# Placing the shift rows of the softmax: from SyncE's queue to ScalarE's, with two transfers of four rows for each group of heads

## The chip, the cores and the metric

The kernel runs on one core of one Trainium2 chip. The metric is the device time of one execution in microseconds (us). A core has five engines, each with its own instruction stream: TensorE (matrix products), VectorE, ScalarE, GpSimd and SyncE (here it only issues DMAs). They wait for each other by semaphores. A DMA is issued by an instruction in the stream of some engine: if an earlier instruction of that stream waits, the issue waits too.

## The reference

One transformer block on 16 sequences of 512 tokens by 512 channels, in float32:

```python
x = x + layernorm(attention(layernorm(x)))     # 32 heads of 16, causal, rotary, biases on q, k, v, o
x = x + layernorm(ffn(layernorm(x)))           # 512 -> 1408 -> 512, silu(gate) * up, ternary weights with scales
```

Inside the attention the weights are softmax(q k^T / 4) over the keys up to the query's position.

## The kernel before

There are two phases, one after the other. The attention (`attention_phase`) goes over the 16 sequences and writes its result to DRAM; the feed-forward part then reads it. The change is in the attention alone.

**Steps.** A sequence has NS = 40 steps: NG = 8 groups g of four heads, each with NU = 5 units u, so step s = 5 g + u. Each engine has a `body(i)` that lists its work for the 40 steps in a fixed order, written out by hand. In it lie, interleaved, work of three sequences: projections of the next sequence, the attention of this one, the output of the one before. Sequences 1 to 13 are passes of a hardware loop; the first and the last ones are written out.

**Heads in slots.** Each head of q and k is held as 64 rows (a slot, SLOT = 64): 48 rows are the 16 dimensions three times over, as high and low float16 halves, and 16 (DH) are constant rows. Two heads (j = 0, 1) stand one above the other in the 128 partitions of `qT` and `kT`; the first index behind the partition is the channel tile ct = g // 2, the second the pair of heads. The halves come from VectorE and are sent to a DRAM buffer `slots` (`send_slots`, four DMAs), then read back in the new order (`fetch_slots`, two DMAs of 256 KB), since rows have to change partitions. Both stand in SyncE's queue. A fetch waits until its sends have landed. The constant rows of k hold 32768 (SHIFT_UNIT), those of q hold 0. They are written to DRAM once, in the set-up.

**Maxima and shift.** Ten steps ahead (AHEAD) of its use, TensorE computes the scores with queries in the partitions (`maxima`, line 799), and VectorE masks them and takes their row maxima (line 674). After the five units of a group, VectorE makes two float16 numbers of each maximum, divided by -32768 (`shift_of_maxima`). At u = 1 of the group before, TensorE turns them into rows (`turn_shift`, line 837), eight rows of 512: four heads, a high and a low one each. ScalarE copies them from PSUM to the tile `shift_rows` (`read_shift`, line 532). Then they are put in two of the constant rows of each head's slot in `qT`, over zeros: `place_shift`, lines 362 to 371, four DMAs of 2 KB at u = 2 in SyncE's queue. The second product, with keys in the partitions (`transposed_scores`, line 813), so has the shift in it, and ScalarE can exponentiate at once (`exponential`, line 526). At u = 0 of a group the second product waits for the shift rows:

```python
                if u == 0:
                    pe.wait_ge(shift_in, 64 * (NG * i + g + 1))
                wait_if_any(pe, ts_read, NS * i + n)
```

The second product has one buffer, `ts`: the next unit's can't start before ScalarE has read it (`ts_read`). The first product has two, `mx`.

**Order on SyncE.** In each step: the placement (u = 2), then a fetch, then a send, then now and then a load or a store of a whole sequence (1 MB). Fetches stand in steps 0, 1, 6, 10, 25, 26, 31 and 35, sends in steps 0, 5, 9, 24, 25, 30, 34 and 39. The key slots of the first channel tile are fetched in step 26 and wanted in step 30.

**Order on ScalarE.** In each step the exponential; a bias (`add_bias`, line 513); a high half (`high_of_roped`, line 520); at u = 1 `read_shift`; at u = 2 the copy of the weighed values (`read_weighed`, line 536), for which TensorE's `turn_weighed` waits; then copies of transposed tiles.

Of the kernel before, what the change touches and what calls it, by code (L numbers as in the profile page):

```python
# [45 lines left out]
def held(engine, value):  # L46

    return value if isinstance(value, int) else engine.to_reg(value)


def wait_if_any(engine, semaphore, value):

    if not isinstance(value, int) or value > 0:
        engine.wait_ge(semaphore, value)
# [16 lines left out]
def attention_phase(nc, x, wT, bias_rows, bias_columns, rope_cos, rope_sin, slots, x1):  # L71

    ctx = ExitStack()
    with ctx:
# [124 lines left out]
        SCALES_AT = 2 + SCALE_STEPS  # L199


        NS = NG * NU
        AHEAD = 2 * NU

# [96 lines left out]
        def exists(i):  # L301

            return not isinstance(i, int) or 0 <= i < NB
# [17 lines left out]
        @block.sync  # L321
        def _(sp):
            sp.dma_start(xn[:, :, :], x[0, :, :, :]).then_inc(x_in, 16)
            for n in range(4):
                sp.dma_start(staged[:, n, :, :], wT[n]).then_inc(weights_in[n], 16)
            for n in range(2):
                sp.dma_start(bias_sb[:, n, :], bias_rows[n]).then_inc(tables_in, 16)
            sp.dma_start(bias_columns_sb[:, :, :], bias_columns).then_inc(tables_in, 16)
            sp.dma_start(cos_sb[:, :], rope_cos).then_inc(tables_in, 16)
            sp.dma_start(sin_sb[:, :], rope_sin).then_inc(tables_in, 16)  # L330
            sp.dma_start(xr[:, :, :], x[0, :, :, :]).then_inc(xr_in, 16)
            sp.wait_ge(padding, 4)
            for n in range(2):
                sp.dma_start(slots[n, :, 3 * DH:SLOT, :].rearrange("jp r t -> r jp t"),
                             half[0:SLOT - 3 * DH, n, 0:1, :].broadcast_to([SLOT - 3 * DH, 8, T])).then_inc(pads_out, 16)

            def send_slots(i, n):

                ct, which = divmod(n, 2)
                b = n % 2  # L340
                halved, fetched = held(sp, 8 * i + n + 1), held(sp, 32 * (NC * i + ct))
                sp.wait_ge(qk_lo, halved)
                wait_if_any(sp, k_in if which else q_in, fetched)
                rows = slots[which, :, 0:3 * DH, :].rearrange("jp (e d s) t -> e jp d (s t)", e=2, s=3)
                both_at, high_at = ((slice(0, 2 * T), slice(2 * T, 3 * T)), (slice(T, 3 * T), slice(0, T)))[which]
                for e in range(2):
                    part = slice(64 * e, 64 * e + 64)
                    sp.dma_start(rows[e][:, :, both_at], half[part, b, :, :]).then_inc(slots_out, 16)
                    sp.dma_start(rows[e][:, :, high_at], half[part, b, 0, :]).then_inc(slots_out, 16)

            def fetch_slots(i, n):

                ct, which = divmod(n, 2)
                dst, arrived = ((qT, q_in), (kT, k_in))[which]
                sp.wait_ge(slots_out, 64 * (8 * i + n + 1))
                if isinstance(i, int) and i == 0 and n < 2:
                    sp.wait_ge(pads_out, 32)
                for j in range(2):
                    sp.dma_start(dst[SLOT * j:SLOT * (j + 1), ct, :, :],
                                 slots[which, 4 * j:4 * j + 4, :, :].rearrange("p r t -> r p t")).then_inc(arrived, 16)  # L360

            def place_shift(i, g):

                turned_rows, placed = held(sp, NG * i + g + 1), held(sp, 64 * (NG * i + g))
                sp.wait_ge(shift_read, turned_rows)
                wait_if_any(sp, shift_in, placed)
                for j in range(2):
                    for pair in range(2):
                        at = 4 * j + 2 * pair
                        sp.dma_start(qT[SLOT * j + 3 * DH:SLOT * j + 3 * DH + 2, g // 2, 2 * (g % 2) + pair, :],  # L370
                                     shift_rows[at:at + 2, g % 2, :]).then_inc(shift_in, 16)

            def body(i):
                for s in range(NS):
                    g, u = divmod(s, NU)
                    if u == 2 and exists(i + (g + 1) // NG):
                        place_shift(i + (g + 1) // NG, (g + 1) % NG)
                    if s in FETCHED_AT and exists(i + FETCHED_AT[s][1]):
                        fetch_slots(i + FETCHED_AT[s][1], FETCHED_AT[s][0])
                    if s in SENT_AT and exists(i + SENT_AT[s][1]):  # L380
                        send_slots(i + SENT_AT[s][1], SENT_AT[s][0])
                    if s == 16 and exists(i + 1) and (not isinstance(i, int) or i + 2 < NB):
                        sp.wait_ge(xT_full, NC * (i + 2))
                        sp.dma_start(xn[:, :, :], x[i + 2, :, :, :]).then_inc(x_in, 16)
                    if s == 26 and exists(i - 1):
                        sp.wait_ge(x1_ready, NT * i)
                        sp.dma_start(x1[i - 1, :, :, :], xr[:, :, :]).then_inc(x1_out, 16)
                    if s == 28 and exists(i - 1) and exists(i):
                        sp.wait_ge(x1_out, 16 * i)
                        sp.dma_start(xr[:, :, :], x[i, :, :, :]).then_inc(xr_in, 16)  # L390

            body(-1)
            body(0)
            with sp.Fori(1, NB - 2) as i:
                body(i)
            body(NB - 2)
            body(NB - 1)
            body(NB)
            sp.wait_ge(x1_out, 16 * NB)
# [100 lines left out]
        def _(act):  # L500
# [26 lines left out]
                                     scale=exp_scale[:, 0:1]).then_inc(ts_read, 1)  # L527

            def read_shift(i, g):
                wait_if_any(act, shift_in, 64 * (NG * i + g - 1))  # L530
                act.wait_ge(shift_full, NG * i + g + 1)
                nc.scalar.activation(shift_rows[0:8, g % 2, :], xb16[0:8, bank_of("s", g), 0:T], ACT.Copy).then_inc(shift_read, 1)

            def read_weighed(i, g):
                act.wait_ge(av_full, NG * i + g + 1)
# [2 lines left out]
            def body(i):  # L538
                for s in range(NS):
                    g, u = divmod(s, NU)  # L540
                    if u == 0 and s in BIASED_AT and exists(i + BIASED_AT[s][1]):
                        add_bias(i + BIASED_AT[s][1], BIASED_AT[s][0])
                    if exists(i):
                        exponential(i, g, u)
                    if u != 0 and s in BIASED_AT and exists(i + BIASED_AT[s][1]):
                        add_bias(i + BIASED_AT[s][1], BIASED_AT[s][0])
                    if s in HIGH_AT and exists(i + HIGH_AT[s][1]):
                        high_of_roped(i + HIGH_AT[s][1], HIGH_AT[s][0])
                    if u == 1 and exists(i + (g + 1) // NG):
                        read_shift(i + (g + 1) // NG, (g + 1) % NG)  # L550
                    if u == 2 and exists(i + (g - 1) // NG):
                        read_weighed(i + (g - 1) // NG, (g - 1) % NG)
                    if s in TRANSPOSED_AT and exists(i + TRANSPOSED_AT[s][2]):
                        kind, c, owner = TRANSPOSED_AT[s]
                        (high_of_x if kind == "x" else high_of_attention)(i + owner, c)

            act.wait_ge(setup_step, SCALES_AT)
            for n in range(4):
                nc.scalar.activation(w_hi[:, n, :, :], staged[:, n, :, :], ACT.Copy,
                                     scale=scale[:, n:n + 1]).then_inc(weights_hi, 1)  # L560
            act.wait_ge(pads_out, 32)
            act.wait_ge(setup_done, 4)
            body(-1)
            body(0)
# [7 lines left out]
        def _(dve):  # L572
# [93 lines left out]
            def maxima(i, n):  # L666
                g, u = divmod(n, NU)
                filled = held(dve, NS * i + n + 1)
                dve.wait_ge(consts, 7)
                dve.wait_ge(mx_full, filled)  # L670
                for pair, qt, at in QUERIES_OF_UNIT[u]:
                    for j in range(2):
                        scores = mx[:, 2 * (n % 2) + j, at:at + P * (qt + 1)]
                        last = nc.vector.tensor_tensor_reduce(  # L674
                            out=scores, in0=scores, in1=causal[:, T - P * (qt + 1):T], scale=1.0, scalar=-3e38,
                            op0=ALU.add, op1=ALU.max, accum_out=row_max[:, g % 2, qt, j, pair:pair + 1])
                last.then_inc(mx_read, 1)

            def shift_of_maxima(i, g):
# [103 lines left out]
        def _(pe):  # L783
# [20 lines left out]
            def transposed_scores(i, n):  # L804
                g, u = divmod(n, NU)
                ct = g // 2
                if u == 0:
                    pe.wait_ge(shift_in, 64 * (NG * i + g + 1))
                wait_if_any(pe, ts_read, NS * i + n)
                for pair, kt, at in KEYS_OF_UNIT[u]:  # L810
                    for j in range(2):
# [567 lines left out]
```

## Time and profile before

| | |
|---|---|
| median of 3 runs | 3089.23 us |
| the three runs | 3087.83, 3089.23, 3095.59 us |
| the profiled execution: its time | 3092.81 us |
| its span, first to last instruction | 3091.1 us |
| mean granted clock of TensorE | 0.938 |
| attention phase, shift placements | first 90.9 us, last 2017.3 us |
| shift placements | 512 DMAs of 2.0 KB |

The profile is of one execution. Its page gives the busy time of each engine; other views give what an engine waited for, the instructions in order of time with the idle time before each and what ended it, and busy time by stretch. PE is TensorE's matrix products, DVE is VectorE, ACT ScalarE, POOL GpSimd, SPq SyncE's queue. Line numbers are those of the kernel before. The granted clock is 1.00 at 2.4 GHz and 0.50 at 1.2 GHz.

### The profile page before, as it was taken

To read this page: it belongs to the slowest core of one execution; us is meant where nothing else is said; L and a number is where in the kernel's file an instruction comes from. 1 tells how busy PE (TensorE), PEld (TensorE's weight loads), DVE (VectorE), ACT (ScalarE), POOL (GpSimd) and SP (SyncE) were. 2 spreads that over 40 slices of the span, in tenths; PEclk is the share of its full clock that TensorE was granted. 3 is DMA by queue.
4 is the path that set the end of the run, shared out by engine and by line. 5 is a ranking of instruction groups with operands and counts; after the bars stand their busy time and mean duration, and the time that the engine had idled before them with its cause. 6 is when DMAs were issued, how large, how long until landed. Compare 5 with 4: busy or idle time off the path is not lost. (4 is left out here: it accounts for less than half of the span.)

```text
span 3091.1 us, 58855 instructions
## 1 busy us (share of the span) xinstructions
PE 2605.4 (84%) x19584; PEld 1263.9 (41%) x19584; DVE 2202.2 (71%) x6495; ACT 1330.2 (43%) x1710; POOL 1020.9 (33%) x1051
## 2 busy tenths in 40 slices
PE   3788888888888888888888888843999999999997
PEld 2343434444434444444444444311444444444443
DVE  4888878788788887887888888836555555545544
ACT  2455555555545555555555555524222222222222
POOL 3454455454544644545446545310000000000000
PEclk9899999999899998998999999876999999999999
DMA  3222232322332323223223232221111111111111
GB/s 140 83 78 90 83 94 63 108 90 64 109 92 77 98 63 104 90 63 111 91 75 97 71 96 77 75 116 56 42 54 41 68 53 42 68 41 54 68 41 41
DMA packets 125076, 237.06 MB, mean 77 GB/s; under 512 B 11408, under 2 KB 94608, under 8 KB 111632
## 3 DMA queue, kind: packets, MB, share of 16 engines
q1 hardware_dynamic: 124816, 233.63, 23.8%
q8 instruction: 158, 2.59, 0.4%
q14 instruction: 102, 0.84, 0.1%
HBM read 148.39 MB, written 84.15 MB: 75 GB/s over the span
## 5 line engine op out<-in xcount | busy, mean ns | idle before, releaser
L674 DVE CUSTOM_DVE_ANT_0 mx<-mx,causal 128x512 f32<-128x512 f32 (+3 forms) x2048 | 944.3, 517 | 245.8 <-PE mx L799 243.5
L526 ACT ACTIVATE probs<-ts,exp_scale 128x1024 f32<-128x1024 f32 x640 | 712.5, 1113 | 714.3 <-PE ts L813 713.9
L452 POOL TENSOR_SCALAR_AFFINE_SELECT probs<-probs 128x512 f32<-128x512 f32 x512 | 320.7, 644 | 782.1 <-ACT probs L526 782.1
L1219 DVE SCALAR_TENSOR_TENSOR hidden<-gu,up_scale,silu 128x512 f32<-128x512 f32 x176 | 131.9, 749 | 418.4 <-PE gu L1269 418.4
L1078 ACT ACTIVATE silu<-gu,gate_scale 128x512 f32<-128x512 f32 x176 | 120.9, 687 | 631.7 <-PE gu L1269 631.7
L799 PE MATMUL mx<-kT,qT 64*128 64x512 f16 (+3 forms) x2048 | 262.6, 315 | 153.5 <-DMA kT<-slots 70.0
L1053 POOL TENSOR_TENSOR f_rstd<-f_var,f_neg_half 128x4 f32<-128x4 f32 x32 | 32.3, 1009 | 929.6 <-DVE f_var L1196 647.5
L813 PE MATMUL ts<-qT,kT 64*128 64x512 f16 (+3 forms) x2048 | 257.5, 310 | 74.2 <-DMA qT<-shift_rows 61.8
L1267 PE MATMUL gu<-f_xT_hi,gate_hi 128*128 128x512 f16 x704 | 267.9, 381 | 52.2 <-issue 52.2
L827 PE MATMUL xb<-probs,vs 128*32 128x512 f32 (+3 forms) x4096 | 309.7, 444 | 1.4 <-POOL probs L452 1.1
L674 DVE DVE_READ_ACCUMULATOR2_ANT row_max<- 128x1 f32 x2048 | 283.3, 138 | 0.0
L1269 PE MATMUL gu<-f_xT_lo,gate_hi 128*128 128x512 f16 x704 | 267.8, 380 | 0.0
L1267 PE MATMUL gu<-f_xT_hi,up_hi 128*128 128x512 f16 x704 | 267.3, 380 | 0.0
L1269 PE MATMUL gu<-f_xT_lo,up_hi 128*128 128x512 f16 x704 | 267.1, 379 | 0.0
L1281 PE MATMUL down<-down_hi,hid_hi 128*128 128x512 f16 x704 | 266.8, 379 | 0.0
L1285 PE MATMUL down<-down_hi,hid_lo 128*128 128x512 f16 x704 | 266.8, 379 | 0.0
L431 POOL TENSOR_TENSOR turned<-biased,sin_sb 64x512 f32<-64x512 f32 x128 | 193.2, 1509 | 161.8 <-ACT biased L513 159.4
L785 PE MATMUL xb<-xT_hi,w_hi 128*128 128x512 f16 x512 | 205.4, 401 | 14.6 <-DVE aT_lo L645 10.3
L799 PEld LDWEIGHTS mx<-kT,qT 64*128 64x128 f16 x2048 | 69.3, 94 | 356.5 <-issue 242.9
L785 PE MATMUL xb<-w_hi,xT_hi 128*128 128x128 f16 x1024 | 207.1, 238 | 5.3 <-DVE aT_lo L645 4.5
L786 PE MATMUL xb<-w_lo,xT_hi 128*128 128x128 f16 x1024 | 206.8, 238 | 0.0
L787 PE MATMUL xb<-w_hi,xT_lo 128*128 128x128 f16 x1024 | 206.1, 238 | 0.0
(145 smaller groups left out, 4607.4 us busy)
## 6 DMA issues: line engine op xcount, KB each, us to landing
slots<-half SPq DMA_DIRECT2D x258, 128.0 KB, 13.7
qT<-slots SPq DMA_DIRECT2D x128, 256.0 KB, 3.8
kT<-slots SPq DMA_DIRECT2D x128, 256.0 KB, 3.8
xn<-x SPq DMA_DIRECT2D x16, 1024.0 KB, 4.9
xr<-x SPq DMA_DIRECT2D x16, 1024.0 KB, 5.8
slots<-half SPq DMA_DIRECT2D x256, 64.0 KB
x<-xr SPq DMA_DIRECT2D x16, 1024.0 KB, 5.6
f_xn<-x SPq DMA_DIRECT2D x16, 1024.0 KB, 4.8
```

What stands on the lines that cost most here:

```text
L452: nc.gpsimd.affine_select(out=d, in_=d, compare_op=ALU.is_ge, fill=0.0, base=0, pattern=[[0, HG], [1, P]], channel_multiplier=-1).then_inc ...
L526: nc.scalar.activation(probs[:, g % 2, u, :, :], ts[:, :, :], ACT.Exp, scale=exp_scale[:, 0:1]).then_inc(ts_read, 1)
L674: last = nc.vector.tensor_tensor_reduce(out=scores, in0=scores, in1=causal[:, T - P * (qt + 1):T], scale=1.0, scalar=-3e38, op0=ALU.add, o ...
L785: nc.tensor.matmul(out, a_hi, b_hi, start=first, stop=False)
L786: nc.tensor.matmul(out, a_hi, b_lo, start=False, stop=False)
L799: last = nc.tensor.matmul(mx[:, 2 * (n % 2) + j, at:at + P * (qt + 1)], qT[rows, ct, p, P * qt:P * (qt + 1)], kT[rows, ct, p, 0:P * (qt + ...
L813: last = nc.tensor.matmul(ts[:, j, at:at + T - P * kt], kT[rows, ct, p, P * kt:P * (kt + 1)], qT[rows, ct, p, P * kt:T], start=True, stop= ...
L827: last = nc.tensor.matmul(bank[32 * h:32 * h + 32, P * kt:T], vs[:, g // 2, kt, HG * (g % 2) + h, :], probs[:, g % 2, u, j, at:at + T - P ...
L1267: nc.tensor.matmul(gu[:, bank, :], hi[:, c, cols], xT_hi[:, c, :], start=c == 0, stop=False)
L1269: last = nc.tensor.matmul(gu[:, bank, :], hi[:, c, cols], xT_lo[:, c, :], start=False, stop=end and not with_rest)
L1281: nc.tensor.matmul(down[:, t, :], hid_hi[:, b % 3, rows], down_hi[:, b, :], start=b == 0, stop=False)
L1285: last = nc.tensor.matmul(down[:, t, :], hid_lo[:, b % 3, rows], down_hi[:, b, :], start=False, stop=b == NI - 1)
```

## The change

The shift rows are issued by ScalarE, at u = 1, directly behind its copy of them, after a wait for that copy. For this the rows of a pair of heads, even and odd, have to be four adjacent partitions of `qT`: the even head's slot gets its constant rows at its end (partitions 48 to 63), the odd head's at its beginning (64 to 79), so that partitions 62 to 65 (`SHIFT_ROWS`) take them. In DRAM a slot has 80 rows, constants on both sides of the data, and a fetch takes rows 16 to 79 or 0 to 63 (`ROWS_OF`). The maxima are stored with the pair ahead of j, so that the eight rows come in this order. The constant rows are sent by four DMAs of 16 rows in place of two.

```diff
+        ROWS_OF = (slice(DH, DH + SLOT), slice(0, SLOT))
+        SHIFT_ROWS = slice(SLOT - 2, SLOT + 2)
...
             for n in range(2):
-                sp.dma_start(slots[n, :, 3 * DH:SLOT, :].rearrange("jp r t -> r jp t"),
-                             half[0:SLOT - 3 * DH, n, 0:1, :].broadcast_to([SLOT - 3 * DH, 8, T])).then_inc(pads_out, 16)
+                for first in (0, SLOT):
+                    sp.dma_start(slots[n, :, first:first + DH, :].rearrange("jp r t -> r jp t"),
+                                 half[0:DH, n, 0:1, :].broadcast_to([DH, 8, T])).then_inc(pads_out, 16)
...
-                rows = slots[which, :, 0:3 * DH, :].rearrange("jp (e d s) t -> e jp d (s t)", e=2, s=3)
+                rows = slots[which, :, DH:SLOT, :].rearrange("jp (e d s) t -> e jp d (s t)", e=2, s=3)
...
-                                 slots[which, 4 * j:4 * j + 4, :, :].rearrange("p r t -> r p t")).then_inc(arrived, 16)
-
-            def place_shift(i, g):
-
-                turned_rows, placed = held(sp, NG * i + g + 1), held(sp, 64 * (NG * i + g))
-                sp.wait_ge(shift_read, turned_rows)
-                wait_if_any(sp, shift_in, placed)
-                for j in range(2):
-                    for pair in range(2):
-                        at = 4 * j + 2 * pair
-                        sp.dma_start(qT[SLOT * j + 3 * DH:SLOT * j + 3 * DH + 2, g // 2, 2 * (g % 2) + pair, :],
-                                     shift_rows[at:at + 2, g % 2, :]).then_inc(shift_in, 16)
+                                 slots[which, 4 * j:4 * j + 4, ROWS_OF[j], :].rearrange("p r t -> r p t")).then_inc(arrived, 16)
...
-                    if u == 2 and exists(i + (g + 1) // NG):
-                        place_shift(i + (g + 1) // NG, (g + 1) % NG)
...
+            def place_shift(i, g):
+                act.wait_ge(shift_read, NG * i + g + 1)
+                wait_if_any(act, shift_in, 32 * (NG * i + g))
+                for pair in range(2):
+                    act.dma_start(qT[SHIFT_ROWS, g // 2, 2 * (g % 2) + pair, :],
+                                  shift_rows[4 * pair:4 * pair + 4, g % 2, :]).then_inc(shift_in, 16)
...
                         read_shift(i + (g + 1) // NG, (g + 1) % NG)
+                        place_shift(i + (g + 1) // NG, (g + 1) % NG)
...
-                            op0=ALU.add, op1=ALU.max, accum_out=row_max[:, g % 2, qt, j, pair:pair + 1])
+                            op0=ALU.add, op1=ALU.max, accum_out=row_max[:, g % 2, qt, pair, j:j + 1])
...
-                    pe.wait_ge(shift_in, 64 * (NG * i + g + 1))
+                    pe.wait_ge(shift_in, 32 * (NG * i + g + 1))
...
-    slots = nc.dram_tensor("slots", (2, 8, SLOT, T), F16, kind="Internal").ap()
+    slots = nc.dram_tensor("slots", (2, 8, SLOT + DH, T), F16, kind="Internal").ap()
```

The waits for `shift_in` and `pads_out` elsewhere have their counts changed to match.

## Rows read from the trace of the kernel before

**Rows 1.** The page: busy us (share of the span) and instructions by engine.
```profile
PE 2605.4 (84%) x19584; PEld 1263.9 (41%) x19584; DVE 2202.2 (71%) x6495; ACT 1330.2 (43%) x1710; POOL 1020.9 (33%) x1051
```

**Rows 2.** What TensorE waited for: us in total, times, longest us.
```profile
PE mx L799 <- DMA kT<-slots: 70.0, 15, 9.7
PE ts L813 <- DMA qT<-shift_rows: 61.8, 30, 5.7
PE mx L799 <- issue: 54.3, 14, 6.2
...
PE ts L813 <- ACT probs L526: 11.7, 15, 1.3
```

**Rows 3.** TensorE in order of time: start us, us, instruction, [idle before <-releaser].
```profile
110.83 0.61 PE L813 MATMUL ts<-qT,kT 64*128 64x512 f16 x2 [5.67 <-DMA qT<-shift_rows]
...
302.43 0.61 PE L813 MATMUL ts<-qT,kT 64*128 64x512 f16 x2 [2.25 <-DMA qT<-shift_rows]
...
1036.98 0.61 PE L799 MATMUL mx<-kT,qT 64*128 64x512 f16 x2 [3.87 <-DMA kT<-slots]
...
1039.56 0.61 PE L813 MATMUL ts<-qT,kT 64*128 64x512 f16 x2 [1.97 <-DMA qT<-shift_rows]
...
1085.00 0.61 PE L813 MATMUL ts<-qT,kT 64*128 64x512 f16 x2 [4.25 <-DMA qT<-shift_rows]
...
1457.20 0.39 PE L813 MATMUL ts<-qT,kT 64*128 64x512 f16 x2 [1.10 <-DMA qT<-shift_rows]
...
1904.35 0.61 PE L813 MATMUL ts<-qT,kT 64*128 64x512 f16 x2 [2.07 <-DMA qT<-shift_rows]
...
1948.70 0.61 PE L813 MATMUL ts<-qT,kT 64*128 64x512 f16 x2 [4.34 <-DMA qT<-shift_rows]
```

**Rows 4.** SyncE's queue in order of time, steps 26, 27 and 40 to 42.
```profile
1032.04 1.28 SPq L359 DMA_DIRECT2D kT<-slots  x2
...
1034.07 3.75 SPq L370 DMA_DIRECT2D qT<-shift_rows  x4
...
1072.07 1.30 SPq L359 DMA_DIRECT2D qT<-slots  x2
1073.59 0.62 SPq L348 DMA_DIRECT2D slots<-half  x1
...
1079.20 1.86 SPq L359 DMA_DIRECT2D kT<-slots  x2
1081.25 2.58 SPq L370 DMA_DIRECT2D qT<-shift_rows  x4
```

**Rows 5.** ScalarE in order of time: step 27, then steps 41 and 42.
```profile
1025.77 1.11 ACT L526 ACTIVATE probs<-ts,exp_scale 128x1024 f32<-128x1024 f32 x1 [2.90 <-PE ts L813]
...
1071.83 0.57 ACT L532 ACTIVATE shift_rows<-xb 8x512 f16<-8x512 f16 x1
1073.08 1.11 ACT L526 ACTIVATE probs<-ts,exp_scale 128x1024 f32<-128x1024 f32 x1 [0.68 <-PE ts L813]
1074.10 0.68 ACT L513 ACTIVATE biased<-xb,bias_qk 128x512 f32<-128x512 f32 x1
1075.40 0.60 ACT L536 ACTIVATE oT<-xb 128x512 f32<-128x512 f32 x1 [0.62 <-PE xb L827]
```

**Rows 6.** Line 370, the placement: duration ns minimum/median/maximum, first and last start us.
```profile
L370 SPq DMA_DIRECT2D qT<-shift_rows x512: 562/563/1568, 90.9 to 2017.3; - x171
```

**Rows 7.** VectorE in order of time, behind the waits of 1039.56 and 1085.00 us.
```profile
1043.25 0.70 DVE L674 CUSTOM_DVE_ANT_0 mx<-mx,causal 128x512 f32<-128x512 f32 x1 [2.95 <-PE mx L799]
...
1088.98 0.70 DVE L674 CUSTOM_DVE_ANT_0 mx<-mx,causal 128x512 f32<-128x512 f32 x1 [3.87 <-PE mx L799]
```

**Rows 8.** Stretches, step 5 to 10: us; PE, PEld, DVE, ACT, POOL busy; clock; DMA.
```profile
1080.40:1099.70 19.30, 14.70 (x139) 8.52 (x140) 14.49 (x52) 8.44 (x11) 8.22 (x10) 0.82 0.29 76
1455.70:1470.20 14.50, 12.33 (x139) 6.97 (x138) 14.15 (x52) 8.60 (x11) 8.30 (x10) 1.00 0.25 66
```

**Rows 9.** A stretch around step 30: us; TensorE busy; granted clock; DMA share, GB/s.
```profile
1035.80:1042.60 6.80, 3.65 (x28) 0.50 0.67 241
```

**Rows 10.** TensorE's second product of step 43 (u = 3).
```profile
1075.49 0.38 PE L813 MATMUL ts<-qT,kT 64*128 64x384 f16 x4
```

More of the change, by code:

```diff
@@ L356, in fetch_slots @@
                 if isinstance(i, int) and i == 0 and n < 2:
-                    sp.wait_ge(pads_out, 32)
+                    sp.wait_ge(pads_out, 64)
                 for j in range(2):
                     sp.dma_start(dst[SLOT * j:SLOT * (j + 1), ct, :, :],
-                                 slots[which, 4 * j:4 * j + 4, :, :].rearrange("p r t -> r p t")).then_inc(arrived, 16)
-            def place_shift(i, g):
-                turned_rows, placed = held(sp, NG * i + g + 1), held(sp, 64 * (NG * i + g))
-                sp.wait_ge(shift_read, turned_rows)
-                wait_if_any(sp, shift_in, placed)
-                for j in range(2):
-                    for pair in range(2):
-                        at = 4 * j + 2 * pair
-                        sp.dma_start(qT[SLOT * j + 3 * DH:SLOT * j + 3 * DH + 2, g // 2, 2 * (g % 2) + pair, :],
-                                     shift_rows[at:at + 2, g % 2, :]).then_inc(shift_in, 16)
+                                 slots[which, 4 * j:4 * j + 4, ROWS_OF[j], :].rearrange("p r t -> r p t")).then_inc(arrived, 16)
             def body(i):
@@ L529, in read_shift @@
             def read_shift(i, g):
-                wait_if_any(act, shift_in, 64 * (NG * i + g - 1))
+                wait_if_any(act, shift_in, 32 * (NG * i + g - 1))
                 act.wait_ge(shift_full, NG * i + g + 1)
                 nc.scalar.activation(shift_rows[0:8, g % 2, :], xb16[0:8, bank_of("s", g), 0:T], ACT.Copy).then_inc(shift_read, 1)
+            def place_shift(i, g):
[4 more added lines that the diff above has]
+                                  shift_rows[4 * pair:4 * pair + 4, g % 2, :]).then_inc(shift_in, 16)
             def read_weighed(i, g):
@@ L560, in _ @@
                                      scale=scale[:, n:n + 1]).then_inc(weights_hi, 1)
-            act.wait_ge(pads_out, 32)
+            act.wait_ge(pads_out, 64)
             act.wait_ge(setup_done, 4)
```

## The prediction
> **What bounds the kernel now.** I read the shares of the page first. TensorE is busy 84% of the span, VectorE 71%, ScalarE 43% [rows 1]. No engine is full, so the time is made of work plus waits on TensorE and VectorE, which run nearly level; ScalarE has room. The second view is what TensorE waited for [rows 2]. Three entries stand out: 70.0 us for the key slots (15 times), 61.8 us for the shift rows (30 times) and 54.3 us with no releaser (14 times, at the return to the loop's head). Only the second is touched by this change.
>
> The third view is where the 30 waits lie [rows 3]. One in each sequence comes at step 30, just after the wait for the key slots: 2.25 us in the first row of this kind, 1.97 at 1039.56 us, 2.07 in the last, so 15 of about 2.0 make some 30 us. The other 32 us lie in the other 15 waits, nearly all at step 5 (a new group of heads, g = 1), and they are uneven: 1.10 us at 1457.20, 4.25 at 1085.00, 5.67 and 4.34 in the first and last large ones. Seven are above 2 us, about 27 us together.
>
> The fourth view is SyncE's queue around such a wait [rows 4]. The shift rows were ready early: ScalarE began the copy at 1071.83 and it took 0.57 us, so 1072.40 [rows 5]. But SyncE issued them only at 1081.25: ahead in its order stood a fetch of query slots (1072.07), four sends (from 1073.59), and a fetch of key slots, which could not go before its sends had landed (1079.20). The four transfers took 2.58 us to issue, and TensorE started at 1085.00, 1.17 us after the last. At step 30 it is the same: the placement stands behind a fetch of key slots and a store, from 1034.07, and took 3.75 us. So the shift rows are late because they queue on SyncE, not because they are slow.
>
> **The change, part by part.**
>
> Taken from SyncE: 4 issues for each of 128 groups, 512 x 563 ns = 288 us [rows 6], and its wait for the copy. SyncE's other work is bound by halves coming from VectorE and by landings. The fetch that makes the 70.0 us wait (step 26) has no placement between itself and its two sends, so I give the 288 us no value. The bounds are 0 and, if the fetch moved up by one placement, 2.58 us x 15 = 39 us gained [rows 2, 4]; I take 0.
>
> The wait that goes: with the placement on ScalarE directly behind the copy, the rows are issued from 1072.40. Two issues and the 1.17 us landing put them in qT at about 1074.7, where TensorE wants them at 1080.75 (1085.00 less 4.25). That is 6 us to spare. All 30 waits go. What they were worth is not the same at both places:
> - Step 30: behind the wait VectorE was idle as well, 2.95 us before its next block of maxima at 1043.25 [rows 7]. So TensorE's 1.97 us moves VectorE forward too. 15 x 2.0 = 30 us. If VectorE took it back, as at the next place, 0 to 10 would be left.
> - Step 5: VectorE is behind TensorE there. The stretch from the maxima of step 5 to those of step 10 takes 14.5 us where the stall was 1.10 us, with VectorE busy 14.15 of it, and 19.3 us where it was 4.25, with VectorE busy 14.49 [rows 8]. So 14.5 us is the floor, set by VectorE; the small stalls cost nothing, and a large one gives back somewhat more than itself (19.3 - 14.5 = 4.8), since the clock was at its lower level after it (0.82 against 1.00 in these two rows). For the seven large ones, 27 us of wait, I take 24 us, as some of it is below the floor. The small ones: 0.
>
> The clock: around step 30 there is a stretch of 6.8 us at 0.50, the 1.2 GHz level, with TensorE busy 3.65 us in it [rows 9]. It begins in the wait for the key slots, which stays, but the wait that goes lies in its middle. If the clock is back up for all that work, 3.65 / 2 = 1.8 us is saved, in 15 sequences 27 us; if it is not, 0. Nearest to a sequence like that is the same one with its key wait of 3.87 us still there, so I take the low end, 0.5 us each, 8 us.
>
> What of the late 4.25 us is issue time? SyncE's four issues took 2.58 us, from 1081.25, and stood 8.85 us behind the copy's end [rows 4, 5]; two issues on ScalarE take 1.13. The Trainium skill speaks against the change here: "DMA: Bandwidth & Descriptors", in "Rules for kernel authors", says that spreading DMAs over the issuing engines does not help bandwidth, as all run on the same 16 DMA engines, and saves issue time only. By that rule alone the sum would hold nothing but the issue time (rival C); by the rows the larger part is what stands ahead in SyncE's order, a fetch that waits for its sends.
>
> Added to ScalarE: a wait for its own copy and two issues, at each of 128 groups, in front of the exponential of step u = 2. No ScalarE issue stands in this trace. The lower bound is 0 (where the engine would have been idle anyhow); the nearest row is SyncE's issue of the same kind, 563 ns, and the far end is its longest, 1568 ns [rows 6]. I take 563 ns and 0.1 us for the wait for the copy: 1.23 us. In a tight group ScalarE stands idle 0.68 us between the copy and that exponential, which comes 0.55 us late. Behind it are queued a bias (0.68 us) and the copy of the weighed values, which now waits 0.62 us for TensorE [rows 5]: the 0.55 is just swallowed. On TensorE's side, the scores of step u = 3 start at 1075.49 [rows 10], and this exponential ends at 1074.19: 1.30 us of room against 0.55. In other groups the exponential waits longer for TensorE anyhow, 2.90 us in one [rows 5]; I count five of eight as tight. For trifles above the cover I put 0.3 us per sequence, 5 us. With 1568 ns issues it is 3.24 us, the exponential 2.56 late, and TensorE 1.3 to 1.9 us late in some five of eight groups: 1.6 x 5 x 16 = 128 us lost. That is the upper bound of the cost.
>
> The other edits: the fetched block has the same 64 rows of 1 KB, now from a stride of 80 rows; the maxima are written at other addresses of the same small tile; the constant rows are sent by four transfers in place of two, during the set-up, while ScalarE is busy with the weights. 0; the set-up could lose a microsecond.
>
> Sum: 30 + 24 + 8 - 5 = 57 us of the profiled execution's 3092.81 us (span 3091.1): 3036. The median of before is 3089.23, 3.6 us lower, and the profiled execution lies inside the three runs (3087.83 to 3095.59). I forecast 3036 us.
>
> **The rivals.**
>
> A. VectorE takes the gain back at step 30 as it does at step 5. For it: it was busy 71% over the whole and has 14.15 of 14.5 in the stretch shown. Against: its 2.95 us idle right behind the wait. It would leave 24 + a third of 30, less 5: 29 us, so 3063.
>
> B. The other side: ScalarE's issues are slow. The place is the exponential of u = 2, on the single score buffer that TensorE refills. The price is 128 us less the 62 gained: 3158 us at the far end. It decides where 62 us are lost in 80 tight groups, 0.78 us each: a stay of 0.68 + 0.62 + 0.78 = 2.08 us for wait and issues, 1.0 us an issue. Against it: median and minimum of 512 issues are 563 and 562 ns.
>
> C. The shift rows still come late, since they share the DMA engines with the slot traffic, and only issue time is saved: 2.58 - 1.13 = 1.45 us [rows 4, 6] at each of 22 large waits (15 + 7), 32 us, less 5: 3066. For it: one placement took 3.75 us at 1034.07, behind other traffic [rows 4]. Against: the 6 us to spare. The skill's rule above would have it so.
>
> D. The clock gives more: stretches at the low level disappear at step 30 too, and the key slots' wait is shorter with SyncE free. 57 + 20 to 30: 3010.
>
> **How the numbers follow.** The forecast 0.55, its own range 3025 to 3048. A 0.13, B 0.07, C 0.10, D 0.15. The range 3008 to 3072 holds the forecast, D, A and most of C. What a measurement can tell from no change is 0.3%, 9 us. Slower than 3098: nearly all of B, 0.07. Within 9 us: the edges of B and C, 0.05. Faster: 0.88.
>
> **What would show it.** TensorE's wait for shift rows falls from 61.8 us to under 5, its wait for key slots stays near 70, and the one at the loop's head near 54. The stretch from step 5 to step 10 is 14.5 us in each sequence. SyncE issues no shift rows; ScalarE has 256 issues of about 0.56 us. TensorE's waits for the exponentials, now 11.7 us [rows 2], stay under 20. I am wrong if the issues on ScalarE last over 1 us, if the key-slot wait grows by what the shift wait loses, or if VectorE's share of a sequence is at its limit.

## The result, and the profile after

The changed kernel takes 3050.51 us, the median of 4 runs (3043.4 to 3056.82), against 3088.9 us before on the same occasion. The ratio is 0.9871 (95% interval 0.984 to 0.9901): 1.3% faster, about 40 us, 31 to 49 by the interval. Forecast were 3036 us and a range of 3008 to 3072. The median lies in that range, 2.5 us above the narrower one that the prediction gave the forecast itself (3025 to 3048). The profiled execution took 3045.72 us, 47.1 us under the one before, and 4.8 us under the median of its kernel; what the profile shows has to be read with that in mind.

The page after, where [rows 1] stands before:

```profile
PE 2582.9 (85%) x19584; PEld 1250.2 (41%) x19584; DVE 2205.0 (72%) x6495; ACT 1328.8 (44%) x1710; POOL 1023.4 (34%) x1051
```

What TensorE waited for (us in total, times, longest us), to be held against [rows 2]:

```profile
PE mx L799 <- DMA kT<-slots: 74.6, 14, 9.3
PE mx L799 <- issue: 57.2, 15, 6.5
...
PE xb L785 <- DVE aT_lo L645: 30.5, 34, 2.0
...
PE xb L860 <- DVE attn L699: 12.7, 26, 1.0
PE ts L813 <- ACT probs L518: 11.5, 13, 1.3
```

What matters is what isn't there: no row for the shift rows, 61.8 us before. The waits for the key slots and at the loop's head are where they were. Waits for small results of VectorE took some of the room (`aT_lo` was 16.3 us).

What VectorE waited for, of the two kernels; first before, then after:

```profile
DVE mx L674 <- PE mx L799: 243.5, 200, 12.5
...
DVE roped L651 <- ACT biased L513: 15.8, 41, 5.4
```

```profile
DVE mx L674 <- PE mx L799: 180.1, 136, 12.1
...
DVE roped L651 <- ACT biased L505: 33.4, 38, 5.3
```

VectorE starves less behind TensorE, by 63 us, and waits 17.6 us longer for ScalarE's bias, a row that the prediction had not looked at.

The placement on ScalarE (line 530): duration ns minimum/median/maximum. Then ScalarE in order of time in steps 41 and 42, to be held against [rows 5]:

```profile
L530 ACTq DMA_DIRECT2D qT<-shift_rows x256: 584/595/1182, 83.1 to 1965.9; - x128
```

```profile
1046.61 0.57 ACT L524 ACTIVATE shift_rows<-xb 8x512 f16<-8x512 f16 x1
1047.29 1.29 ACTq L530 DMA_DIRECT2D qT<-shift_rows  x2
1048.69 1.11 ACT L518 ACTIVATE probs<-ts,exp_scale 128x1024 f32<-128x1024 f32 x1 [1.51 <-DMA qT<-shift_rows]
1049.71 0.68 ACT L505 ACTIVATE biased<-xb,bias_qk 128x512 f32<-128x512 f32 x1
1050.32 0.60 ACT L535 ACTIVATE oT<-xb 128x512 f32<-128x512 f32 x1
```

The issues last 595 ns, the stay between copy and exponential is 1.51 us, and the copy of the weighed values no longer waits for TensorE: the 0.62 us of cover before it is used up.

Where the time went, by sequence. The table is worked out from the starts of line 799's products at the steps named, as means over the 12 sequences from the third on, 299.6 to 1777.8 us before and 291.7 to 1741.1 us after:

| us | step 30 to 31 | 31 to 40, loop's head | 0 to 5 | 5 to 10 | 10 to 20 | 20 to 30 | sum | of it at the low clock |
|---|---|---|---|---|---|---|---|---|
| before | 5.73 | 26.26 | 13.52 | 15.40 | 29.02 | 33.25 | 123.18 | 16.5 |
| after | 3.54 | 26.24 | 14.29 | 14.53 | 28.72 | 33.45 | 120.78 | 11.6 |

Step 30 gave back 2.19 us and steps 5 to 10 0.87, but steps 0 to 5 took 0.77 us of it. Those 12 sequences hold 28.8 us of the 47.1; the rest lies in the first and last ones, which had large stalls too. Over all sequences, worked out in the same way, step 30 gave 31.1 us and steps 5 to 10 gave 25.2, steps 0 to 5 took 12.4, and everything else together gave 3.2.

### The profile page after: what moved, and what is told of

It is laid out like the page before. It is cut to its first block and busy times, and to the rows that moved or that the text cites. A ratio compares the mean times of both kernels' runs of the same rounds, so it can differ in the third digit from the quotient of the medians.

```text
span 3044.0 us, 58497 instructions
## 1 busy us (share of the span) xinstructions
PE 2582.9 (85%) x19584; PEld 1250.2 (41%) x19584; DVE 2205.0 (72%) x6495; ACT 1328.8 (44%) x1710; POOL 1023.4 (34%) x1051
## 5 line engine op out<-in xcount | busy, mean ns | idle before, releaser
L799 PE MATMUL mx<-kT,qT 64*128 64x512 f16 (+3 forms) x2048 | 262.0, 314 | 163.0 <-DMA kT<-slots 74.6
L813 PE MATMUL ts<-qT,kT 64*128 64x512 f16 (+3 forms) x2048 | 257.3, 309 | 11.8 <-ACT probs L518 11.5
L785 PE MATMUL xb<-w_hi,xT_hi 128*128 128x128 f16 x1024 | 197.5, 232 | 18.3 <-DVE aT_lo L645 17.5
L786 PE MATMUL xb<-xT_lo,w_hi 128*128 128x512 f16 x512 | 201.7, 394 | 0.0
L787 PE MATMUL xb<-xT_hi,w_lo 128*128 128x512 f16 x512 | 201.4, 393 | 0.0
```

Of the source, the lines that this page charges most:

```text
L785: nc.tensor.matmul(out, a_hi, b_hi, start=first, stop=False)
L786: nc.tensor.matmul(out, a_hi, b_lo, start=False, stop=False)
L799: last = nc.tensor.matmul(mx[:, 2 * (n % 2) + j, at:at + P * (qt + 1)], qT[rows, ct, p, P * qt:P * (qt + 1)], kT[rows, ct, p, 0:P * (qt + ...
L813: last = nc.tensor.matmul(ts[:, j, at:at + T - P * kt], kT[rows, ct, p, P * kt:P * (kt + 1)], qT[rows, ct, p, P * kt:T], start=True, stop= ...
```

## The experiments

Twelve kernels were run, 5 to 12 executions each. Each was compared with executions of the kernel before on its own chip, whose medians were 3089.3 us (beside e1 to e4), 3092.24 (e0, e7 to e9), 3090.03 (e5, e6, e10) and 3092.33 (e11).

| kernel | median us | ratio to before (95%) |
|---|---|---|
| e1: two transfers, SyncE, u = 2 | 3087.77 | 0.9993 (0.9983 to 1.0003) |
| e2: four transfers, ScalarE, u = 1 | 3096.36 | 1.0016 (1.0004 to 1.0027) |
| e3: two, ScalarE, u = 3 | 3059.91 | 0.9902 (0.9886 to 0.9919) |
| e4: two, SyncE, u = 1, ahead of the fetch | 3053.25 | 0.9883 (0.9865 to 0.9901) |
| e0: the changed kernel again | 3051.74 | 0.9867 (0.9844 to 0.989) |
| e10: before, sends ahead of fetches | 3035.74 | 0.9825 (0.9808 to 0.9842) |
| e7: changed, sends ahead | 2986.03 | 0.9659 (0.9637 to 0.9681) |
| e9: e3, sends ahead | 2971.27 | 0.9613 (0.9595 to 0.9631) |
| e8: e4, sends ahead | 2973.6 | 0.9602 (0.9584 to 0.962) |
| e5: changed, light statistics | 3042.82 | 0.9845 (0.9825 to 0.9865) |
| e6: before, light statistics | 3090.56 | 1.0 (0.9988 to 1.0011) |
| e11: changed, light normalisation | 3038.51 | 0.9819 (0.9792 to 0.9846) |

### The parts of the change: layout, engine, place in the order

**e1** keeps the new layout and two transfers, but leaves them where they were in SyncE's queue.

```diff
-                    act.dma_start(...)            # ScalarE, u == 1
+                    if u == 2 and exists(i + (g + 1) // NG):      # SyncE, ahead of fetch and send of the step
+                        place_shift(i + (g + 1) // NG, (g + 1) % NG)
```

> The new layout and two transfers of four rows, but issued by SyncE at u = 2 in the old place. Theory (the rows are late through SyncE's order, issue time is the smaller part): the issue of a placement falls from 2.58 to some 1.2 us, so each large wait for shift rows loses about 1.4 us: the total falls from 61.8 us to 25 to 35, and the time by 20 to 30 us, to 3060 to 3070. Rival (the transfers themselves are what is late): nearly all of the change's gain, 3045 to 3055. Rival (issue time is hidden): 3085 to 3090.

TensorE's waits in e1, and its placement (duration ns minimum/median/maximum):

```profile
PE mx L802 <- DMA kT<-slots: 66.3, 15, 8.1
...
PE ts L816 <- DMA qT<-shift_rows: 51.3, 29, 5.4
```

```profile
L373 SPq DMA_DIRECT2D qT<-shift_rows x256: 577/663/1657, 89.6 to 2007.5; - x128
```

The wait fell by 10.5 us only, and the time not measurably. The theory's numbers were missed: half the issues are worth 10 us of wait, not 27 to 37, and the time stays above its window. One reason is that a four-row issue took 663 ns on SyncE and not 563, so that a placement lost 0.93 us of issue time (4 x 563 less 2 x 663 ns). The rival "issue time is hidden" has the time. Layout and number of transfers alone bring nothing that can be measured. Rival C of the prediction, rows still late and only issue time saved, is refuted by both kernels: the changed one has no wait left, and issue time alone gives nothing.

**e4** has the same two transfers in SyncE's queue, one step earlier, so that they stand ahead of the fetch of the key slots.

```diff
-                    if u == 2 and exists(i + (g + 1) // NG):
+                    if u == 1 and exists(i + (g + 1) // NG):
                         place_shift(i + (g + 1) // NG, (g + 1) % NG)
```

> The new layout with two transfers, issued by SyncE, but at u = 1 and ahead of the fetch of that step, so ahead of the fetches of steps 1, 6, 26 and 31. Theory (order, not the engine): TensorE's wait for shift rows is under 10 us, ScalarE carries nothing, and the time is 3030 to 3045. Rival (SyncE has to be left, since a placement that waits for ScalarE's copy now holds up the fetches behind it): the wait for the key slots grows by 1 us or more in each sequence and the time is 3060 to 3085.

TensorE's waits in e4, and SyncE's queue before a step 30, to be held against [rows 4]: the placement now stands between the sends and the fetch of the key slots.

```profile
PE mx L802 <- DMA kT<-slots: 65.6, 14, 9.5
...
PE ts L816 <- DMA qT<-shift_rows: 1.6, 1, 1.6
```

```profile
1021.09 1.37 SPq L373 DMA_DIRECT2D qT<-shift_rows  x2
1023.31 1.32 SPq L364 DMA_DIRECT2D kT<-slots  x2
```

The wait for the shift rows is gone but for one of 1.6 us, and the interval of the ratio, 0.9865 to 0.9901, holds the changed kernel's 0.9871 and 0.9867. The time is 8 us above the expected window's top and 7 us under the rival's bottom; the wait for the key slots did not grow. So the mechanism is shown: what made the rows late was their place in SyncE's order, and one step up on the same engine takes the wait away as the change of engine does.

**e2** has the old layout with four transfers, on ScalarE, as a double dose of issues.

```diff
+            def place_shift(i, g):
+                act.wait_ge(shift_read, NG * i + g + 1)
+                ...
+                for j in range(2):
+                    for pair in range(2):
+                        act.dma_start(...)        # 2 rows each
```

> The old layout with four transfers of two rows, but issued by ScalarE directly behind its copy, as the change does with two. Theory (the issues on ScalarE delay the exponential and the bias of u = 2, and VectorE waits for that bias, 1.7 us per sequence in the changed kernel): two issues more, 1.2 us, make that wait 3 to 5 us per sequence, and the time is 25 to 45 us above the changed kernel's 3050, 3075 to 3095. Rival (ScalarE's issues are covered): 3045 to 3055.

ScalarE in order of time in e2, then what waited for it:

```profile
1049.01 0.57 ACT L519 ACTIVATE shift_rows<-xb 8x512 f16<-8x512 f16 x1
1049.69 2.38 ACTq L527 DMA_DIRECT2D qT<-shift_rows  x4
1052.19 1.11 ACT L513 ACTIVATE probs<-ts,exp_scale 128x1024 f32<-128x1024 f32 x1 [2.61 <-DMA qT<-shift_rows]
```

```profile
DVE roped L648 <- ACT biased L500: 81.5, 50, 6.2
...
PE ts L810 <- ACT probs L513: 56.2, 84, 2.9
...
PE xb L842 <- ACT oT L532: 43.5, 94, 0.7
```

It is no faster than the kernel before, though its wait for shift rows is gone; its median is 1 us above the theory's window. Against the changed kernel it loses 45 us for two more issues in each group: VectorE's wait for the bias is 81.5 us in place of 33.4, TensorE's for the exponential 56.2 in place of 11.5. This is the mechanism of rival B: it was to decide at a stay of 2.08 us between copy and exponential, and at 2.61 us the whole gain is lost. So the four-row layout, worth nothing in e1, is what makes the move to ScalarE pay: the stay is 1.51 us with it.

**e3** moves the two issues two steps down on ScalarE.

```diff
                     if u == 1 and exists(i + (g + 1) // NG):
                         read_shift(i + (g + 1) // NG, (g + 1) % NG)
-                        place_shift(i + (g + 1) // NG, (g + 1) % NG)
...
+                    if u == 3 and exists(i + (g + 1) // NG):
+                        place_shift(i + (g + 1) // NG, (g + 1) % NG)
```

> The changed kernel with the two issues on ScalarE moved two steps down, behind the exponential of u = 3. Theory: VectorE's wait for the bias of u = 2 goes back to nearly 0, the shift rows are still in time, the stretch of steps 0 to 5 falls from 14.3 us by 0.5 to 1 us, and the time is 8 to 25 us below the changed kernel, 3025 to 3042. Rival (the shortfall against the forecast is the clock's alone): 3045 to 3055. If the rows come late again: the wait for shift rows is back and the time is above 3060.

VectorE's wait for the bias is back at 15.1 us, the shift rows are waited for only 6.8 us, and steps 0 to 5 take 14.0 us in place of 14.3, much as the theory had it. But the median is 8 us above the changed kernel's, above the windows of theory and clock rival alike. The intervals of the two ratios, 0.9886 to 0.9919 here and 0.9844 to 0.989 in e0, overlap by a little, so the loss itself is not certain. What the two profiles differ in is in the next section.

### What the clock does

The loop's 12 sequences as one stretch (us; TensorE busy; granted clock; DMA), before, changed, e0 (the changed kernel again), e3, e4 and e8:

```profile
299.60:1777.80 1478.20, 1233.35 (x11330) 0.93 0.30 87
```

```profile
291.70:1741.10 1449.40, 1214.37 (x11328) 0.95 0.31 89
```

```profile
294.30:1749.40 1455.10, 1226.56 (x11330) 0.94 0.31 89
```

```profile
295.30:1756.10 1460.80, 1240.30 (x11328) 0.93 0.30 88
```

```profile
293.90:1761.90 1468.00, 1254.67 (x11328) 0.92 0.30 88
```

```profile
285.50:1679.80 1394.30, 1205.27 (x11330) 0.97 0.32 93
```

The first two rows say something about the change too: of the 28.8 us that it saves in these sequences, 19.0 are TensorE's busy time, the same work at a higher mean clock, and only 9.8 are idle time, though the waits for shift rows in these sequences came to about 40 us. Other waits took part of their place.

e3 and e4 wait less than the changed kernel: TensorE idles 220.5 and 213.3 us in these rows, against 235.0 (228.5 in e0). But it is busy 26 and 40 us longer than in the changed kernel's profile, 14 and 28 longer than in e0's, at the same work and a mean clock of 0.93 and 0.92. In 10 of the 12 sequences of e4 and in 6 of e3, but in 1 of the changed kernel's and in 4 of e0's, a stretch at the low clock falls into steps 10 to 20, which then take 30.3 us against 28.6, as these two rows show (e4, then the changed kernel):

```profile
964.50:994.80 30.30, 26.83 (x210) 0.94 0.23 66
```

```profile
1070.40:1099.00 28.60, 25.15 (x211) 1.00 0.23 70
```

The runs of one kernel scatter by as much: the changed kernel took 3043.74 us at a mean clock of 0.949 and 3061.64 at 0.942, with nothing else known to differ. At a like clock, e4 (3052.0 and 3052.2 us at 0.941 and 0.940) is 3 to 10 us better than the changed kernel (3055.3, 3059.7 and 3061.6 at 0.942), e3 (3061.0 and 3063.6 at 0.942) is not; the chips differ, and so few runs are a hint and no more. **e0**, the changed kernel once more on another chip, has its level again.

> The changed kernel again, on the same chip as the runs beside it. Expected 3043 to 3057, TensorE's low clock 10 to 14 us per sequence. If its level on this chip is that of the two kernels without shift waits run before (3053 and 3060), the three don't differ.

Its ratio is 0.9867, beside 0.9871 for the first runs. By the intervals it is not told from e4. What places a low stretch in steps 10 to 20 more often in one kernel than in the other was not found; no run here fixes it.

### Does VectorE set the pace?

**e5 and e6** lighten VectorE in steps 0 to 3, in the changed kernel and in the one before.

```diff
-                nc.vector.bn_stats(stats[:, t, :], xn[:, t, :]).then_inc(ln1_step, 1)
+                nc.vector.bn_stats(stats[:, t, :], xn[:, t, 0:64]).then_inc(ln1_step, 1)
```

> The changed kernel with VectorE's statistics of the next x over 64 columns in place of 512 (the variance of x is so left out of the result; the time is read for the load only): some 0.5 us less on VectorE in each of steps 0, 1, 2 and 3. Theory (with the waits gone VectorE sets the pace of steps 0 to 5 and 5 to 10): the two stretches, 14.3 and 14.5 us, lose 1 to 2 us together, and the time falls by 12 to 30 us from 3051 to 3021 to 3039. Rival (TensorE and its clock set it): within 6 us of 3051.

> The same lighter statistics in the kernel before. Theory (there the shift rows' arrival sets step 5): steps 0 to 5 get shorter, the wait for shift rows grows from 61.8 us by what they lose, and the time falls by under 10 us from 3090. Rival (VectorE's load is worth the same in both kernels): 12 to 30 us less, 3060 to 3078.

In the kernel before nothing is gained (3090.56 us), as the theory had it, but not by its mechanism: steps 0 to 5 did not get shorter (14.0 us on the mean of the 12 sequences, 13.52 before), and the wait for shift rows did not grow:

```profile
PE ts L813 <- DMA qT<-shift_rows: 57.0, 29, 6.1
```

In the changed one the median is 9 us lower, 4 us short of the theory's window and outside the rival's, with an interval that overlaps e0's; its runs reach from 3034.41 to 3064.33 us. The profiled one is the slowest of them, and its two stretches are 14.51 and 14.60 us on the mean, not shorter. So nothing in steps 0 to 5 bears the theory out. They go by TensorE's clock: before, the same five steps took 12.3 us at the full clock and 14.8 us at 0.80 (us; PE, PEld, DVE, ACT, POOL busy; clock):

```profile
1068.10:1080.40 12.30, 12.08 (x102) 5.33 (x102) 12.04 (x41) 7.83 (x10) 6.02 (x6) 1.00 0.36 102
1193.60:1208.40 14.80, 14.59 (x100) 5.72 (x100) 12.27 (x41) 7.71 (x10) 5.90 (x6) 0.80 0.40 114
```

**e11** lightens VectorE in steps 6 to 8.

```diff
-                nc.vector.tensor_scalar(xn[:, t, :], xn[:, t, :], mv[:, t, 0:1], rstd[:, t:t + 1],
+                nc.vector.tensor_scalar(xn[:, t, 0:64], xn[:, t, 0:64], mv[:, t, 0:1], rstd[:, t:t + 1],
```

> The changed kernel with VectorE's normalisation of the next x over 64 of its 512 columns (the rest of x goes on unnormalised; the time is read for the load only): four instructions of 0.64 us in steps 6 to 8 become short, some 2 us less on VectorE per sequence. Theory (the floor of 14.5 us from step 5 to step 10 is VectorE's, busy 14.15 of it in the kernel before): that stretch falls to 12.5 to 13.8 us and the time by 10 to 30 us, to 3020 to 3041. Rival (the floor is TensorE's own work and its clock): the stretch stays at 14.5 us and the time within 6 us of 3051.

Steps 5 to 10 in the changed kernel, then in e11:

```profile
1055.90:1070.40 14.50, 12.15 (x138) 6.82 (x140) 14.13 (x53) 8.38 (x11) 8.41 (x10) 1.00 0.25 68
```

```profile
1056.60:1070.30 13.70, 12.22 (x139) 6.87 (x140) 13.33 (x53) 8.39 (x11) 8.35 (x10) 1.00 0.27 70
```

VectorE's busy time falls by 0.80 us and the stretch by as much, with TensorE's work as before: the floor of 14.5 us is VectorE's. The mean of 12 sequences goes from 14.52 us (e0) to 13.64; 0.88 us in 15 sequences is 13 us, and the median fell by 13.2, with an interval that just touches e0's. The expectation's 2 us less on VectorE were counted too high. The shorter instruction, first in e0 and then in e11 (duration ns minimum/median/maximum), saves 0.23 us by the medians:

```profile
L635 DVE TENSOR_SCALAR xn<-xn,mv,rstd x64: 533/540/1289, 11.1 to 1802.0; 128x512 f32<-128x512 f32 x64
```

```profile
L635 DVE TENSOR_SCALAR xn<-xn,mv,rstd x64: 303/309/1058, 11.1 to 1790.0; 128x64 f32<-128x64 f32 x64
```

Four of them make 0.92 us, so nearly all that VectorE lost shows in the stretch.

### A version that beats both

The wait for the key slots is of the same kind. Before step 30, SyncE stands at the fetch of the query slots until their sends have landed, and only then sends the key halves. **e7** puts sends ahead of fetches and gives query and key slots a semaphore each, since their counts would mix otherwise.

```diff
-        slots_out = sem("slots_out")
+        slots_out = [sem("q_slots_out"), sem("k_slots_out")]
...
-                sp.wait_ge(slots_out, 64 * (8 * i + n + 1))
+                sp.wait_ge(slots_out[which], 64 * (NC * i + ct + 1))
...
+                    if s in SENT_AT and exists(i + SENT_AT[s][1]):
+                        send_slots(i + SENT_AT[s][1], SENT_AT[s][0])
                     if s in FETCHED_AT and exists(i + FETCHED_AT[s][1]):
                         fetch_slots(i + FETCHED_AT[s][1], FETCHED_AT[s][0])
-                    if s in SENT_AT and exists(i + SENT_AT[s][1]):
-                        send_slots(i + SENT_AT[s][1], SENT_AT[s][0])
```

> The changed kernel, and in each step SyncE's send ahead of its fetch, with a semaphore of their own for the sent query and key slots. In steps 25 and 0 the key halves' send then goes before SyncE waits for the query slots to land. Theory (the wait for the key slots before step 30 is SyncE's order as well): the wait falls from 75 us to 10 to 35, the time by 35 to 60 us, to 2990 to 3015. Rival (the halves come from VectorE no sooner): the wait stays above 60 us and the time at 3043 to 3057. Rival (the clock takes it back): the wait falls, TensorE's low clock grows from 11.6 us per sequence to 17 or more, and the time is 3025 to 3040.

SyncE's queue at this place, before and in e7:

```profile
1025.74 1.30 SPq L359 DMA_DIRECT2D qT<-slots  x2
1027.21 0.63 SPq L348 DMA_DIRECT2D slots<-half  x1
...
1032.04 1.28 SPq L359 DMA_DIRECT2D kT<-slots  x2
```

```profile
979.78 1.28 SPq L364 DMA_DIRECT2D qT<-slots  x2
982.11 1.23 SPq L364 DMA_DIRECT2D kT<-slots  x2
```

TensorE's wait for it in e7:

```profile
PE mx L799 <- DMA kT<-slots: 39.7, 14, 7.8
```

The key fetch follows the query fetch after 2.33 us in place of 6.30. The wait falls from 74.6 us (70.5 in e0) to 39.7, 5 us above the expected window, and the time by 66 us, more than expected, to 4 us under the window: the mean clock rose too (0.946 in e0's profile, 0.955 here). **e8** and **e9** do the same with the placements of e4 and e3.

> SyncE issues the shift rows at u = 1, as in the run before (3053), and sends go before fetches. Theory: the same gain by the key slots as beside it, and no issue time on ScalarE: 2985 to 3015, at or up to 15 us below the one with ScalarE's placement. Rival (a placement in SyncE's queue that waits for ScalarE holds up the sends behind it): 10 to 30 us above that one.

> ScalarE issues the shift rows behind the exponential of u = 3, and sends go before fetches. Theory: between the two beside it, 2988 to 3015. Rival (clock): as with the same placement before, 8 to 12 us above the one at u = 1.

They take 2973.6 and 2971.27 us, 12 and 15 us under e7, and 11 and 17 us under their windows; e9 does not lie between the other two, as its theory had it. Here the runs of all three have a mean clock of 0.955 to 0.963, and at a like clock the distance is nearly the same: 2986.03 us for e7 at 0.961, 2973.6 for e8 and 2975.23 for e9 at 0.960. So the price of ScalarE's issues in front of the exponential of u = 2 is about 13 us. The rivals that put e8 10 to 30 us and e9 8 to 12 us above e7 are refuted.

**e10** is the kernel before with the sends ahead, to see whether the two waits hide each other.

> The kernel before with sends ahead of fetches and a semaphore each for query and key slots, the shift rows still placed by SyncE at u = 2 in four transfers. Theory (the key slots' wait is independent of the placement's): wait for key slots 32 to 42 us in place of 70, shift rows still waited for, time 50 to 70 us below 3090, 3020 to 3040. Rival (the two waits hide each other, since the placement of step 27 stands behind the fetch of step 26): the wait for shift rows falls with it to under 35 us and the time is below 3015, so most of the change's gain is had without the change. Rival (it grows instead): above 3045.

```profile
PE ts L813 <- DMA qT<-shift_rows: 38.3, 24, 2.7
...
PE mx L799 <- DMA kT<-slots: 27.0, 15, 7.4
```

54 us faster, within the theory's window, shift rows still waited for. But the wait for the key slots is 5 us under the window, and the one for the shift rows fell by 23.5 us with the placement untouched, probably since it stands behind the same fetches: the two waits have a part in common, if a smaller one than the first rival wanted (under 35 us of wait, under 3015 us). The key slots' order alone is worth 54 us, the placement alone 40, both (e7) 106 us. That this is more than the sum, in spite of the common part, goes with the mean clock, 0.943 to 0.945 in the runs of e10 and 0.955 to 0.962 in those of e7; no run separates it.

## Why the prediction was right, point by point

- **The rows are late by SyncE's order.** Right, and shown by e4 and e1: 1.6 us of wait are left when they stand ahead of the fetch, and 51.3 us when only their issues are halved. The Trainium skill's rule, that other engines' queues save issue time only ("DMA: Bandwidth & Descriptors", "Rules for kernel authors"), would leave only the issue time as a gain. By these runs that time is worth 10.5 us of wait and nothing measurable in the total (e1); the rest came from the order in the queue (e4).
- **Nothing for SyncE's freed 288 us.** Right: the wait for the key slots is 74.6 us after, 70.0 before.
- **Step 30, 30 us.** Right: 2.19 us per sequence in the loop and 31.1 us over all. The trace before has 14 such waits and not 15, 27.6 us in all. The clock's part was forecast at 0.5 us beside the 2.0, 8 us in all; TensorE's busy time in this step went from 3.78 us to 3.54, so about 0.2 us of it showed.
- **Step 5, 24 us.** The floor is right and VectorE's (e11), each sequence now takes 14.5 us there, and steps 5 to 10 gave 25.2 us over all sequences. But steps 0 to 5, which the prediction took as unchanged, took 12.4 us back, so that as a gain the term was counted too high. In the loop before, the large stalls came in three sequences whose steps 0 to 5 had run at the full clock, in 12.1 to 12.2 us; where they had run in 14.7 or more, the shift rows were in time. In the changed kernel none of the 12 sequences ran steps 0 to 5 in under 12.9 us. So steps 0 to 10 took 28.92 us on the mean before (13.52 + 15.40) and 28.82 after: in the loop this term was 0.1 us per sequence, not the 1.5 that 24 us in 16 sequences make. The stall and the low clock had stood in for each other. e1 says the same from the other side: with its stalls, these ten steps take 28.44 us. Where a sequence has neither, both are gained: in two sequences of e3 steps 0 to 5 take 12.1 and 12.2 us with no stall behind them, and the ten steps 26.6. That I took the clock of steps 0 to 5 as given is the step that was off.
- **ScalarE, 5 us.** Mis-sized: 13 us (e7 against e8 and e9). The issue was 595 ns, not 563; the stay 1.51 us, not 1.23, so that the exponential of a tight group comes 0.83 us late (1.51 less 0.68) and not 0.55: more than the 0.62 us of cover, though less than the 1.30 us of room on TensorE's side. And the chain left out VectorE, which waits for the bias behind that exponential, 33.4 us against 15.8. Without the sends ahead this price is covered by the clock's scatter (e3).
- **The other side.** Rival B's mechanism was borne out by e2: at 2.61 us the gain was gone. Its point of decision, 2.08 us, lies between that and the 1.51 us of the change; no run stands closer to it.
- **Rival D's half of a sentence**, that the key slots' wait shrinks with SyncE free, is refuted; that wait is SyncE's own order too, and it took e7 to bring it down to 39.7 us.

57 us were forecast between profiled executions, and 47.1 were measured: 31.1 at step 30, 25.2 in steps 5 to 10, 12.4 given back in steps 0 to 5, and 3.2 elsewhere. Between medians 53 us were forecast (3089 to 3036), and 40 (31 to 49) were measured. ScalarE's 13 us and the clock lie within these terms; no run separates their shares. So the mechanism and the large term were right, and the time came out in the range in spite of two terms that were counted wrong, steps 0 to 5 and ScalarE.

## What to carry to other kernels

When a small transfer is late, look first at what stands ahead of it in its issuer's order and what that waits for; moving it one step up on the same engine can do what another engine does (e4). Issues on a computing engine are not free because that engine is 43% busy: count the stay in front of the next instruction, and every engine that waits for what comes behind it. And when a stall appears only in passes that ran fast before it, taking it away gives back less than its length.

## What the runs showed of the hardware

The granted clock of TensorE takes part in every comparison here. In most sequences it fell to its lower level (0.50) after TensorE had idled, at the wait for the key slots and at the loop's head; in the kernel before, for example, at 1158.62 us, within the idle time of 4.90 us that ended at 1161.21, and at 947.00, within the one of 3.40 us that ended at 947.26. And some kernels with fewer waits ran at a lower mean clock (0.92 and 0.93 in e4 and e3 over the loop's 12 sequences, 0.95 and 0.94 in the changed kernel). The same kernel's runs differ by 18 us with the mean clock at 0.942 or 0.949. A difference under 10 us between two such kernels is not told from that by five runs, as e0, e3 and e4 show. A DMA issue on ScalarE took 595 ns for four rows and 571 for two (in e2), on SyncE 563 for two rows and 663 and 646 for four (e1 and e4, all medians), and the first arithmetic on ScalarE behind two of them began 1.51 us after the copy's end, behind four of them 2.61.
